# Attention and mixture-of-experts layer on one Trainium2 core: the written-out orders of its five engines replaced by other orders of the same steps

## Chip, cores and metric

One Trainium2 chip, one of its cores. The metric is the device time of one execution in microseconds (us), the median of several runs. The kernel before has a median of 611.8 us over 3 runs.

## The reference

The input is x of 8 batches, 512 tokens, 128 channels, float32. One layer is computed:

```python
x = x + attention(layernorm(x), wq, wk, wv, wo, head_dirs, scale)
x = x + moe(layernorm(x), ...)

# attention: 16 heads, queries and keys of 3 channels, values of 8, causal
scores = einsum('bhtd,bhsd->bhts', q3, k3) * scale + q_on_dir[..., :, None] * k_on_dir[..., None, :]
out = einsum('bhts,bhsd->bhtd', softmax(where(causal, scores, -inf)), v) @ wo

# moe: one shared expert for every token and the best 2 of 8 experts, hidden width 512
shared = gelu(xf @ Wfc_s + bfc_s) @ Wproj_s + bproj_s
routed = sum over e of (gelu(xf @ Wfc[e] + bfc[e]) @ Wproj[e] + bproj[e]) * gate[:, e]
```

## The kernel before

**Steps.** The work is cut into steps, each a few instructions of one engine. A step is written as kind.b.n, with b a batch (or a group of batches in the expert part) and n a part. Five tables give the order in which each engine issues its steps: TENSOR_ORDER (TensorE, PE in the profile), SCALAR_ORDER (ScalarE, ACT), VECTOR_ORDER (VectorE, DVE), POOL_ORDER (GpSimd, POOL) and SYNC_ORDER (SyncE, SP, which only issues DMAs). In the first, "@place" names the PSUM bank or banks of the step, out of 8: `HB.1.5@5` is in bank 5, and a score step with two pairs of banks has two digits, `E.7.6@64` being banks 4, 5 and banks 6, 7. One place, as in `M.3.1@0`, means banks 0 and 1 for most score steps.

**Attention of one batch.** S1 and N1 normalize (DVE, POOL), T1 and XE transpose, QKV projects. QK splits queries and keys into three bfloat16 parts (DVE), SK and SQ spread them (POOL), TK, TQ, KE and QE transpose them, and the DMA step KP writes keys into a padded tile. Softmax maxima come first: each M step (matmuls of L1382 and L1384) writes scores to PSUM, and the MX step of the same number (DVE, L1062) reduces them to `negmax`; 24 of them a batch. PT (L1071 to L1073) splits the maxima of a head group, TM and QM put them into the queries. Then E (L1396, L1404) computes scores with the maxima subtracted, EX (ACT, L920) takes the exponential, MK (POOL, L789) masks, PV (L1423) multiplies by the values, and OE, TP, DV, TO, HE, PJ and RS bring the result back to `acc`.

**Expert part.** S2, N2, T2, X2, RL, LG, LX, RT, RK and RC route a batch: RT picks two experts, RK and RC (L1139 to L1145) give each token a row in a table, SC (POOL, L813) sends rows there by indirect DMA. The shared expert is H, GS, Y and SA; BS (POOL, L800) adds its bias. Batches form three groups of 5, 2 and 1. TB (DVE, L1154 to L1170) makes the group's table of blocks from the counts that CT (L1474) adds up. Then come 47, 23 and 15 blocks of 128 rows: WC (SP, L627) loads the 578 KB of a block's weights into one of 6 `wcur` buffers, XB (SP, L640) a pair of blocks' rows into one of 2 `xblk` buffers, XT and XV transpose, HB (L1502) and GB (ACT, L958) are the first product and the gelu, YB (L1510) and YE (DVE, L1241) the second, YS (SP, L647) stores the pair. GA (POOL, L827) fetches rows back and CB (DVE, L1258) adds them. The last group is summed on TensorE instead (SB on DVE, CM on PE, L1526). OU (SP, L652) stores results.

**What sets the order.** Every engine issues its table's steps strictly in order, and a step waits with semaphores for what it reads. The waits come out of the tables: `counted()` numbers the steps of each kind as the tables have them, and `banks_before()` finds for each PE step who held its banks before, and `wait_taken` waits until that was read:

```python
for kind, b, n, place in TENSOR:
    for unit in sorted(BEFORE.get((kind, b, n), ())):
        wait_taken(unit)
...
elif kind == "HB":
    pe.wait_ge(gelu_blk, nth("GB", b, n))
```

So a step on a bank waits for the engine that empties it. SP's queue is in order too: XB behind a WC stands still while that WC waits for its `wcur` buffer:

```python
if k >= NW:
    pg, ps = block_at(k - NW)
    sp.wait_ge(yblk_done, nth("YB", pg, ps))
    sp.wait_ge(yblk_ready, nth("YE", pg, ps // 2))
    sp.wait_ge(gelu_blk, nth("GB", pg, ps))
```

ACT's function tables (ACT_TABLE_LOAD) are loaded whenever an Exp step follows a gelu step or the other way round, so the order in SCALAR_ORDER sets their number.

Of the kernel before, what the change touches and what calls it, by code (L numbers as in the profile page):

```python
# [1657 lines left out]
```

## Time and profile before

| | |
|---|---|
| median of 3 runs | 611.8 us (611.73 to 622.73) |
| the profiled execution | 612.41 us, its span 610.2 us |
| mean granted TensorE clock | 0.988 of full speed |
| busy: PE, PEld, DVE, ACT, POOL | 550.8, 423.7, 436.3, 388.0, 325.1 us |
| DMA | 99.48 MB, mean 163 GB/s |
| chain that ended last | PE 64%, DVE 19%, issue 7%, ACT 4%, DMA 3% |

The span is that of one execution on the core; 2.2 us of its time lie outside it. PE is the matmuls, PEld the weight loads that overlap them. The chain is followed back from the last instruction to whatever released each step.

### The profile page before, as it was taken

How to read it: one execution, taken by the hardware profiler on the slowest of the kernel's cores; microseconds unless marked ns; L12 is line 12 of the kernel's file. 1: busy time of each engine (PE TensorE's matmuls, PEld its weight loads, DVE VectorE, ACT ScalarE, POOL GpSimd, SP SyncE). 2: the span in 40 equal slices, each digit the busy share in tenths (PEclk: the TensorE clock that was granted, in tenths of full speed). 3: DMA queues.
4: the chain of work that ended last, by engine and by line, in shares of the span. 5: the costliest groups of instructions: out<-in, count | busy, mean ns of one | idle time of the engine just before them, and what ended most of it. 6: DMA issues, size and time to landing. Idle time of an engine off the chain costs nothing.

```text
span 610.2 us, 15780 instructions
## 1 busy us (share of the span) xinstructions
PE 550.8 (90%) x5276; PEld 423.7 (69%) x5318; DVE 436.3 (72%) x1147; ACT 388.0 (64%) x685; POOL 325.1 (53%) x434
## 2 busy tenths in 40 slices
PE   2688999998998999999899998999999899998997
PEld 2555556675664756656668887889878678888996
DVE  6799987799889797798974742446653235845888
ACT  5346678675657679758578686857795945543342
POOL 6844635678268576779654222210450574674544
PEclk9999999999999999999999998999999989998999
DMA  6235752031372212002435858577868846797993
GB/s 179 48 98 173 247 179 98 18 105 36 109 197 81 61 34 74 27 28 49 150 106 200 281 164 275 192 226 226 253 204 287 261 149 196 232 338 249 287 286 120
DMA packets 62429, 99.48 MB, mean 163 GB/s; under 512 B 9020, under 2 KB 47840, under 8 KB 61920
## 3 DMA queue, kind: packets, MB, share of 16 engines
q1 hardware_dynamic: 58512, 90.62, 47.7%
q0 software_dynamic: 3840, 7.87, 3.9%
q8 instruction: 44, 0.72, 0.5%
q14 instruction: 33, 0.27, 0.1%
HBM read 83.37 MB, written 31.80 MB: 189 GB/s over the span
## 4 chain that ended last, share of the span: by engine, by line
PE 64%; DVE 19%; issue 7%; ACT 4%; DMA 3%; SPq 1%; POOL 1%; DVEq 0%; ACTq 0%; POOLq 0%
PE banks L1502 11%; PE banks L1510 11%; PE banks L1423 9%; DVE negmax L1062 7%; PE banks L1333 7%; PE banks L1382 7%; PE banks L1384 4%; PE banks L1480 3%; PE banks L1485 3%; DMA xblk<-xs 2%; ACT probs L920 2%; PE banks L1404 2%; PE banks L1352 2%; PE banks L1526 2%; PE banks L1396 1%
## 5 line engine op out<-in xcount | busy, mean ns | idle before, releaser
L1062 DVE TENSOR_REDUCE negmax<-banks 128x2 f32<-128x1024 f32 (+3 forms) x192 | 193.8, 1039 | 42.2 <-PE banks L1384 40.8
L920 ACT ACTIVATE probs<-banks 128x1024 f32<-128x1024 f32 x160 | 155.6, 1025 | 24.9 <-PE banks L1404 17.0
L789 POOL TENSOR_SCALAR_AFFINE_SELECT probs<-probs 128x512 f32<-128x512 f32 x128 | 78.7, 641 | 128.2 <-ACT probs L920 128.1
L958 ACT ACTIVATE hblk<-banks,wcur 128x128 f32<-128x128 f32 x340 | 95.1, 379 | 80.4 <-PE banks L1502 71.5
L1382 PE MATMUL banks<-kpad,qst 128*128 128x256 bf16 (+3 forms) x470 | 104.9, 295 | 3.9 <-DVE negmax L1062 2.1
L1384 PE MATMUL banks<-future,identb 128*128 128x128 bf16 x512 | 95.6, 220 | 8.5 <-DVE negmax L1062 2.6
L1502 PE MATMUL banks<-xblkT,wcur 128*128 128x128 f32 x680 | 93.0, 285 | 10.0 <-issue 5.9
L1502 PEld LDWEIGHTS banks<-xblkT,wcur 128*128 128x128 f32 x680 | 84.8, 197 | 16.2 <-issue 10.0
L1510 PE MATMUL banks<-wcur,hblk 128*128 128x128 f32 x680 | 91.4, 280 | 1.1 <-ACT hblk L958 1.1
L1510 PEld LDWEIGHTS banks<-wcur,hblk 128*128 128x128 f32 x680 | 83.6, 195 | 5.3 <-issue 3.0
L813 POOL DMA_INDIRECT xs<-x2n,row x64 | 64.6, 1009 | 42.4 <-DVE row L1145 17.6
L1382 PEld LDWEIGHTS banks<-kpad,qst 128*128 128x128 bf16 x512 | 50.0, 98 | 39.7 <-DVE negmax L1062 12.2
L827 POOL DMA_INDIRECT got<-ys,from_row x56 | 55.7, 994 | 40.3 <-DVE acc L1258 21.6
L1423 PE MATMUL banks<-probs,vext 128*32 128x512 f32 (+3 forms) x1024 | 75.7, 436 | 0.2 <-issue 0.2
L1423 PEld LDWEIGHTS banks<-probs,vext 128*32 128x32 f32 x1024 | 30.2, 110 | 45.1 <-issue 36.5
L1384 PEld LDWEIGHTS banks<-future,identb 128*128 128x128 bf16 x512 | 50.3, 98 | 3.5 <-issue 2.3
L884 ACT ACTIVATE ot<-banks 128x512 f32<-128x512 f32 x32 | 19.1, 598 | 49.9 <-PE banks L1423 49.9
L1241 DVE TENSOR_TENSOR yblk<-banks,wcur 128x128 f32<-128x128 f32 x85 | 20.6, 284 | 37.8 <-PE banks L1510 34.3
L1226 DVE COPY xblkT<-banks 128x256 f32<-128x256 f32 (+1 forms) x44 | 18.0, 410 | 28.5 <-PE banks L1333 25.1
L1485 PE MATMUL banks<-w2s,hidden 128*128 128x128 f32 x256 | 34.8, 280 | 0.0
L1480 PE MATMUL banks<-x2T,w1s 128*128 128x512 f32 x64 | 32.4, 611 | 0.0
L1485 PEld LDWEIGHTS banks<-w2s,hidden 128*128 128x128 f32 x256 | 31.0, 192 | 1.7 <-issue 1.3
(156 smaller groups left out, 819.5 us busy)
## 6 DMA issues: line engine op xcount, KB each, us to landing
wcur<-wtab SPq DMA_DIRECT2D x85, 578.0 KB, 5.2
xs<-in_L_attn_x SPq DMA_DIRECT2D x8, 1188.0 KB, 7.1
xblk<-xs SPq DMA_DIRECT2D x85, 64.0 KB
ys<-yblk SPq DMA_DIRECT2D x34, 128.0 KB, 4.0
kpad<-kst SPq DMA_DIRECT2D x64, 64.0 KB, 2.1
xs<-in_L_attn_x SPq DMA_DIRECT2D x8, 505.0 KB
acc<-in_L_attn_x SPq DMA_DIRECT2D x8, 256.0 KB, 5.3
wtab<-in_L_ffn_Wfc SPq DMA_DIRECT2D x2, 1024.0 KB
```

Of the source, the lines that this page charges most:

```text
L789: pool.affine_select(out=v, in_=v, compare_op=ALU.is_ge, fill=0.0, base=0, pattern=[[0, R], [1, P]], channel_multiplier=-1).then_inc(maske ...
L813: pool.indirect_dma_start(out=xs[g % 2], out_offset=bass.IndirectOffsetOnAxis(ap=row[:, b % 2, k, i:i + 1], axis=0), in_=x2n[:, b % NX2, i ...
L827: pool.indirect_dma_start(out=got[:, half_of, k, j, :], out_offset=None, in_=ys[g], in_offset=bass.IndirectOffsetOnAxis(ap=from_row[:, b % ...
L920: nc.scalar.activation(probs[:, g % 2, heads[0]:heads[-1] + 1, at:at + P * sum(EUNITS[unit])], src, ACT.Exp).then_inc(exp_done, 1)
L958: ins = nc.scalar.activation(hblk[:, k % 3, q, :], one(PLACE["HB", g, s])[:, P * q:P * q + P], ACT.Gelu_apprx_tanh, bias=wcur[:, k % NW, 2 ...
L1062: dve.tensor_reduce(negmax[:, g, 0, tiles - 1, heads[0]:heads[-1] + 1], unit_view(PLACE["M", b, n], tiles), AX.X, ALU.max, negate=True).th ...
L1382: mm(dst[:, m, :], qst[:, key_place(b, g), g % 2, P * i:P * i + P], kpad[:, key_place(b, g), g % 2, r, 0:P * tiles], start=opens_bank(tile ...
L1384: ins = mm(dst[:, m, P * i:P * i + P], identb[:], future[:], start=False, stop=True, skip_group_check=True)
L1423: ins = mm(banks[W * r:W * r + W, place, P * j:T], vext[:, j, R * g + r, :], probs[:, g % 2, r, PCOL[NT - j]:PCOL[NT - j] + T - P * j], st ...
L1485: ins = mm(one(place)[:, P * i:P * i + P], hidden[:, q, P * i:P * i + P], w2s[:, q, :], start=(q == 0), stop=(q == NQ - 1))
L1502: ins = mm(one(place)[:, P * q:P * q + P], wcur[:, k % NW, P * q:P * q + P], v, start=True, stop=True)
L1510: ins = mm(one(place)[:, at:at + C], hblk[:, k % 3, q, :], wcur[:, k % NW, HID + C * q:HID + C * q + C], start=(q == 0), stop=(q == NQ - 1))
```

## The change

The five tables are replaced. Every step is there once, as before: 781 on TensorE, 393 on ScalarE, 492 on VectorE, 234 on GpSimd, 228 on SyncE. No function changes. TensorE's steps stand 1.6 places away from their old place on average, at most 21; VectorE's 1.5, one of them 60; GpSimd's 2.4, at most 28; SyncE's 2.9, at most 35; ScalarE's 0.7. Most steps on TensorE are also in other PSUM banks. Since ACT's table loads follow from the order, there are 36 of them now, and 34 before.

Four lines of the diff, two of SYNC_ORDER and two of POOL_ORDER, stand for the rest:

```diff
-    WC.1.22 XB.2.0 WC.2.0 XB.2.1 WC.2.1 XB.2.2 OU.0.1 YS.1.8 YS.1.9 WC.2.2 WC.2.3 WC.2.4 YS.1.10 WC.2.5 XB.2.3
...
+    YS.1.8 WC.1.22 OU.0.0 WC.2.0 XB.2.0 YS.1.9 WC.2.1 XB.2.1 WC.2.2 XB.2.2 WC.2.3 WC.2.4 YS.1.11 WC.2.5 XB.2.3
...
-    GA.1.0 GA.1.1 GA.1.3 N2.7.0 GA.2.3 GA.2.1 GA.2.2 GA.2.0 BS.6.0 BS.7.0 SC.7.2 SC.7.0 SC.7.1 SC.7.3 GA.3.0
...
+    GA.1.3 GA.1.0 GA.1.1 GA.1.2 N2.7.0 GA.2.0 GA.2.2 GA.2.3 GA.2.1 BS.7.0 SC.7.2 SC.7.3 SC.7.1 SC.7.0 GA.3.1
```

BS.6.0 now stands before SC.6.2. In VECTOR_ORDER the first PT (PT.0.0) comes behind 14 MX steps, where it came behind 12. In SCALAR_ORDER `X2.6.0 EX.7.5 EX.7.6 LX.6.0 GB.0.34` becomes `X2.6.0 GB.0.34 LX.6.0 EX.7.5 EX.7.6`. In TENSOR_ORDER `CT.2.0@0 HB.1.12@4 H.7.0@7 H.7.3@2 YB.1.11@3 RK.7.0@7 HB.1.13@4 YB.1.12@1 HB.1.14@7` becomes `CT.2.0@7 HB.1.13@5 RK.7.0@4 YB.1.11@0 HB.1.12@3 H.7.0@5 H.7.3@2 YB.1.12@7 HB.1.14@4`.

**Place 1, VectorE in batch 2.** The last two maxima of batch 2 and the first of batch 3 (MX.3.2), with the two PT steps between them (L1071 to L1073). Before:

```order
L1042 TENSOR_TENSOR parts<-rest 128x2x96
L1062 TENSOR_REDUCE negmax<-banks 128x2 x2
L1071 TENSOR_TENSOR negmax<-negmax 128x16
L1072 COPY qrows<-negmax 128x2x4x4
L1073 TENSOR_TENSOR qrows<-negmax 128x4x4
L1071 TENSOR_TENSOR negmax<-negmax 128x16
L1072 COPY qrows<-negmax 128x2x4x4
L1073 TENSOR_TENSOR qrows<-negmax 128x4x4
L1062 TENSOR_REDUCE negmax<-banks 128x2
L1139 TENSOR_TENSOR row_of<-banks,first_row 128x32
```

and now:

```order
L1042 TENSOR_TENSOR parts<-rest 128x2x96
L1062 TENSOR_REDUCE negmax<-banks 128x2 x2
L1139 TENSOR_TENSOR row_of<-banks,first_row 128x32
L1140 TENSOR_TENSOR row_hot<-hot,row_of 128x64
L1141 TENSOR_REDUCE row_f<-row_hot 128x8
L1145 CAST row<-row_f 128x8
L1071 TENSOR_TENSOR negmax<-negmax 128x16
L1072 COPY qrows<-negmax 128x2x4x4
L1073 TENSOR_TENSOR qrows<-negmax 128x4x4
L1062 TENSOR_REDUCE negmax<-banks 128x2
L1248 TENSOR_TENSOR acc<-banks,acc 128x512
```

The pair of reductions was MX.2.21 and MX.2.15 and is now MX.2.21 and MX.3.2; the step that frees the bank of M.3.2 has moved ahead of both PT steps.

**Place 2, TensorE at the end of batch 7's attention.** L1404 is E.7.6 here, L1423 is PV.7.3, the L1502 rows are blocks of group 1. Before:

```order
L1480 MATMUL banks<-x2T,w1s 128x512
L1502 MATMUL banks<-xblkT,wcur 128x128 x4
L1404 MATMUL banks<-qmst,kpad 128x512 x4
L1502 MATMUL banks<-xblkT,wcur 128x128 x4
L1333 MATMUL banks<-ident,xblk 128x128 x2
L1502 MATMUL banks<-xblkT,wcur 128x128 x8
L1423 MATMUL banks<-probs,vext 32x512 x4
```

and now:

```order
L1502 MATMUL banks<-xblkT,wcur 128x128 x4
L1480 MATMUL banks<-x2T,w1s 128x512
L1502 MATMUL banks<-xblkT,wcur 128x128 x4
L1404 MATMUL banks<-qmst,kpad 128x512 x4
L1423 MATMUL banks<-probs,vext 32x512 x4
L1423 MATMUL banks<-probs,vext 32x384 x4
L1423 MATMUL banks<-probs,vext 32x256 x4
L1423 MATMUL banks<-probs,vext 32x128 x4
L1502 MATMUL banks<-xblkT,wcur 128x128 x4
```

HB.1.4 has moved ahead of E.7.6, and HB.1.5, which stood ahead of PV.7.3, behind it.

**Place 3, SyncE in group 1.** The weights of blocks 1.10 and 1.11 (L627) and the first rows of pair 1.7 (L640). Before:

```order
L627 DMA wcur<-wtab 128x1156
L647 DMA ys<-yblk 128x2x128
L626 TENSOR_LOAD block_of
L626 ISA x2
L627 ISA
L627 DMA wcur<-wtab 128x1156
L639 TENSOR_LOAD block_of
L639 ISA x2
L640 ISA
L640 DMA xblk<-xs 128x128
```

and now, with the weights of block 1.9 in the first row and those of 1.10 in the last:

```order
L627 DMA wcur<-wtab 128x1156
L639 TENSOR_LOAD block_of
L639 ISA x2
L640 ISA
L640 DMA xblk<-xs 128x128
L639 TENSOR_LOAD block_of
L639 ISA x2
L640 ISA
L640 DMA xblk<-xs 128x128
L626 TENSOR_LOAD block_of
L626 ISA x2
L627 ISA
L627 DMA wcur<-wtab 128x1156
```

The loads of pair 1.7 now come before those of the weights of 1.10 and 1.11, which they followed.

## Rows read from the trace of the kernel before

**Rows 1.** The page: busy time of the engines, and the chain's engines.

```profile
PE 550.8 (90%) x5276; PEld 423.7 (69%) x5318; DVE 436.3 (72%) x1147; ACT 388.0 (64%) x685; POOL 325.1 (53%) x434
...
PE 64%; DVE 19%; issue 7%; ACT 4%; DMA 3%; SPq 1%; POOL 1%; DVEq 0%; ACTq 0%; POOLq 0%
```

**Rows 2.** Windows: length; busy PE, PEld, DVE, ACT, POOL; granted clock; DMA share; GB/s.

```profile
0.00:20.00 20.00, 6.38 (x25) 4.87 (x25) 15.13 (x46) 8.75 (x8) 14.46 (x37) 1.00 0.52 146
...
40.00:50.00 10.00, 5.96 (x69) 3.83 (x69) 9.75 (x20) 7.03 (x9) 5.15 (x7) 1.00 0.39 139
...
140.00:150.00 10.00, 9.35 (x97) 6.51 (x95) 9.55 (x34) 6.61 (x8) 8.91 (x12) 1.00 0.15 42
150.00:160.00 10.00, 7.63 (x77) 5.11 (x80) 8.41 (x25) 2.72 (x4) 3.46 (x5) 0.83 0.11 28
...
490.00:500.00 10.00, 10.00 (x99) 6.69 (x98) 2.99 (x9) 5.10 (x18) 6.64 (x9) 0.85 0.44 129
...
540.00:550.00 10.00, 10.00 (x91) 9.94 (x90) 4.95 (x15) 6.24 (x19) 6.84 (x8) 1.00 0.99 344
```

**Rows 3.** Timeline of PE, its long idle times: start, us, instructions, idle before.

```profile
152.32 0.31 PE L1384 MATMUL banks<-future,identb 128*128 128x128 bf16 x1 [2.57 <-DVE negmax L1062]
...
377.50 2.05 PE L1502 MATMUL banks<-xblkT,wcur 128*128 128x128 f32 x8 [2.64 <-ACT hblk L958]
...
489.16 3.41 PE L1502 MATMUL banks<-xblkT,wcur 128*128 128x128 f32 x16 [1.94 <-issue]
...
513.72 0.41 PE L1333 MATMUL banks<-ident,xblk 128*128 128x128 f32 x2 [1.51 <-DMA xblk<-xs]
...
529.87 1.16 PE L1502 MATMUL banks<-xblkT,wcur 128*128 128x128 f32 x8 [1.39 <-DVE row L1145]
...
553.13 0.41 PE L1333 MATMUL banks<-ident,xblk 128*128 128x128 f32 x2 [2.55 <-DMA xblk<-xs]
```

**Rows 4.** Timelines of DVE and POOL from 145 to 151 us.

```profile
146.98 2.09 DVE L1071 TENSOR_TENSOR negmax<-negmax 128x16 f32<-128x16 f32 x1
...
150.92 0.94 DVE L1062 TENSOR_REDUCE negmax<-banks 128x2 f32<-128x768 f32 x1
...
146.26 2.90 POOL L766 COPY krows<-parts 128x576 bf16<-128x576 bf16 x3
```

**Rows 5.** Line L1071 in the whole trace: min/median/max in ns.

```profile
L1071 DVE TENSOR_TENSOR negmax<-negmax x32: 156/167/2091, 38.7 to 465.5; 128x16 f32<-128x16 f32 x32
```

**Rows 6.** Timelines of ACT and SP from 480 to 488 us.

```profile
482.02 5.74 ACT L920 ACTIVATE probs<-banks 128x1024 f32<-128x1024 f32 x6
...
480.29 1.75 SPq L640 DMA_DIRECT2D xblk<-xs  x2
482.90 1.68 SPq L627 DMA_DIRECT2D wcur<-wtab  x2
```

**Rows 7.** The chain from 503 to 514 us: start, us, what.

```profile
503.77 0.50 DVE yblk L1241 x2
...
508.92 4.67 DMA xblk<-xs
```

**Rows 8.** Timelines of DVE and POOL from 524 to 528 us.

```profile
524.33 3.06 DVE L1161 SCALAR_TENSOR_TENSOR end_row<-used,end_row 1x8 f32<-1x8 f32 x1
...
524.87 2.49 POOL L800 TENSOR_TENSOR acc<-acc,b2s 128x512 f32<-128x512 f32 x2
```

**Rows 9.** Timeline of SP from 544 to 549 us.

```profile
544.70 0.34 SPq L627 DMA_DIRECT2D wcur<-wtab  x1
545.89 1.44 SPq L640 DMA_DIRECT2D xblk<-xs  x2
```

**Rows 10.** Timeline of ACT from 435 to 441 us.

```profile
435.62 0.60 ACT L884 ACTIVATE x2T<-banks 128x512 f32<-128x512 f32 x1 [1.06 <-PE banks L1333]
438.33 1.94 ACT L920 ACTIVATE probs<-banks 128x1024 f32<-128x1024 f32 x2 [2.11 <-PE banks L1404]
...
440.40 1.28 ACT L958 ACT_TABLE_LOAD   x1
```

More of the change, by code:

```diff
@@ new lines @@
+    M.3.11@1 M.3.5@7 TQ.3.1@6 E.2.5@4 M.2.16@2 TK.3.1@0 M.2.12@6 M.2.23@1 E.2.1@24 QKV.4.0@0 M.2.14@6 M.2.18@2
+    T2.1.0@1 M.2.22@4 M.2.20@6 RL.1.0@1 H.1.3@3 M.2.19@4 H.1.2@2 H.1.1@1 H.1.0@0 E.2.3@62 M.2.21@4 QKV.4.1@1
+    PV.2.0@0 Y.1.0@7 M.3.2@2 Y.1.1@7 RK.1.0@6 E.2.4@40 Y.1.2@7 M.2.15@2 Y.1.3@7 M.3.0@0 TK.4.0@6 M.3.1@2
+    TK.4.1@7 TM.2.2@5 TM.2.3@4 TP.2.0@6 M.3.3@0 PV.2.1@5 E.2.8@0 M.3.12@2 E.2.6@64 M.3.4@0 E.2.11@2 M.3.14@6
+    TP.2.1@5 M.3.17@4 E.2.9@20 M.3.13@6 M.3.16@4 T1.5.0@3 E.2.10@6 M.3.23@2 M.3.15@4 E.2.7@26 M.3.19@0 M.3.7@4
@@ new lines @@
+    M.7.22@4 YB.0.17@6 HB.0.18@1 TP.6.1@6 M.7.0@2 XT.0.10@0 HB.0.19@5 HB.0.20@4 YB.0.18@7 HB.0.21@3 E.6.8@0
+    XT.0.11@6 M.7.20@4 YB.0.19@7 YB.0.20@3 HB.0.22@6 XT.0.12@7 E.6.7@40 YB.0.21@3 HB.0.23@2 M.7.1@4 PV.6.3@7
+    M.7.2@0 XT.0.13@6 HB.0.24@3 YB.0.22@2 M.7.3@0 PV.6.2@6 YB.0.23@2 HB.0.25@6 XT.0.14@2 YB.0.24@3 M.7.7@0
+    TM.7.0@6 M.7.21@4 HB.0.26@7 HB.0.27@6 YB.0.25@3 E.7.0@40 HB.0.28@2 XT.0.15@6 TP.6.3@3 YB.0.26@7 TP.6.2@2
+    HB.0.29@3 YB.0.27@7 TO.6.0@2 M.7.10@4 E.7.2@0 YB.0.28@2 XT.0.16@7 HB.0.31@6 M.7.6@0 HB.0.30@7 M.7.8@4
@@ new lines @@
+    YB.0.29@2 PJ.6.0@3 HB.0.32@6 HB.0.33@7 E.7.1@20 YB.0.30@5 M.7.17@6 XT.0.17@4 YB.0.31@5 M.7.9@6 HB.0.34@4
+    YB.0.32@5 M.7.13@6 TM.7.1@1 T2.6.0@0 M.7.16@2 YB.0.33@5 RL.6.0@0 XT.0.18@7 H.6.3@6 E.7.3@20 HB.0.35@7
+    PV.7.0@5 M.7.14@0 YB.0.34@4 HB.0.36@3 RK.6.0@2 YB.0.35@4 HB.0.37@7 E.7.4@20 YB.0.36@6 E.7.5@4 XT.0.19@7
+    YB.0.37@6 H.6.0@7 HB.0.38@6 CT.1.0@3 HB.0.39@2 XT.0.20@1 H.6.2@0 TM.7.3@1 HB.0.40@5 HB.0.41@4 YB.0.38@6
+    XT.0.21@2 YB.0.39@6 HB.0.42@5 YB.0.40@6 M.7.15@2 YB.0.41@6 YB.0.42@7 XT.0.23@6 HB.0.43@0 XT.0.22@5 PV.7.1@4
@@ new lines @@
+    VS.2.1 XE.3.0 EX.0.4 EX.0.1 EX.0.0 VS.2.0 EX.0.3 EX.0.2 EX.0.9 EX.0.5 EX.0.6 OE.0.0 EX.0.14 EX.0.7 EX.0.8
+    KE.2.0 OE.0.1 EX.0.12 EX.0.13 EX.0.19 EX.0.10 EX.0.11 KE.2.1 QE.2.0 OE.0.2 EX.0.16 EX.0.15 EX.0.18 EX.0.17
+    EX.1.0 EX.1.1 EX.1.4 OE.0.3 EX.1.3 EX.1.2 HE.0.0 EX.1.6 EX.1.5 EX.1.9 OE.1.0 EX.1.14 EX.1.8 EX.1.7 VS.3.0
+    EX.1.10 EX.1.11 X2.0.0 QE.2.1 VS.3.1 EX.1.13 EX.1.12 OE.1.1 LX.0.0 GS.0.3 GS.0.2 GS.0.1 GS.0.0 OE.1.2
+    EX.1.15 EX.1.16 EX.1.19 EX.1.18 EX.1.17 KE.3.0 OE.1.3 QE.3.0 HE.1.0 XE.4.0 EX.2.0 EX.2.1 EX.2.4 QE.3.1
@@ new lines @@
+    MX.0.11 MX.0.2 MX.0.13 MX.0.5 MX.0.0 MX.0.8 MX.0.16 MX.0.14 PT.0.0 MX.0.10 QM.0.0 MX.0.18 QK.2.1 PT.0.1
+    MX.0.12 QM.0.1 QK.2.0 MX.1.5 MX.0.15 MX.0.17 MX.0.23 PT.0.2 MX.0.19 MX.1.11 S1.4.0 QM.0.2 MX.1.0 DV.0.0
+    MX.0.22 MX.1.4 MX.1.3 MX.0.21 MX.0.20 PT.0.3 MX.1.1 MX.1.2 QM.0.3 DV.0.1 MX.1.12 MX.1.17 MX.1.23 MX.1.14
+    MX.1.18 MX.1.13 PT.1.0 MX.1.16 QM.1.0 DV.0.2 MX.1.6 MX.1.9 MX.1.15 MX.1.8 PT.1.2 MX.1.10 MX.1.7 PT.1.1
+    QM.1.1 DV.0.3 MX.1.20 MX.1.22 QM.1.2 RS.0.0 S2.0.0 MX.2.4 MX.1.19 MX.1.21 PT.1.3 MX.2.1 DV.1.0 QK.3.0
@@ L241 @@
+    YS.1.10 WC.2.6 XB.2.4 WC.2.7 WC.2.8 XB.2.5 OU.2.0 WC.2.9 OU.0.1 WC.2.10 WC.2.11 WC.2.12 OU.3.0 WC.2.13
+    XB.2.6 OU.2.1 OU.5.1 OU.4.1 XB.2.7 OU.4.0 OU.5.0 WC.2.14 OU.1.1 OU.3.1 OU.6.1 OU.6.0 OU.7.1 OU.7.0
 """
```

287 lines of the change are left out of this document (130 added, 157 removed).

## Prediction

> **What bounds the kernel now.** I read the page's busy times first, then the chain by engine, windows of 10 us, the idle times of TensorE in its timeline, and around each of the long ones the timelines of the engine that it waited for. TensorE is the bound: busy 550.8 us of a span of 610.2, and 64% of the chain [rows 1]. Its instructions stay, so what an order can win is the other 59.4 us, and the time lost at the lower clock. Of the 59.4, 13.6 lie in the first 20 us (20 less 6.4 busy) [rows 2], where data arrive and nothing else can be done. Six of the long idle times add up to 2.57 + 2.64 + 1.94 + 1.51 + 1.39 + 2.55 = 12.6 us [rows 3]. The other 33 us are in many mostly small pieces, 4.0 of them between 40 and 50 us [rows 2]. Behind some of the long ones the clock falls: in the windows from 150 and 490 us the granted clock averages 0.83 and 0.85 [rows 2]. With levels of 1.2 and 2.4 GHz, 0.83 means a third of 10 us at the lower, in which half of the work is lost: 1.7 us; at 0.85, 1.5 us. So a long idle time costs up to 1.7 us more than it lasts.
>
> The profiled execution took 612.41 us, 0.6 more than the median of 611.8. I sum against 612.4 and subtract 0.6 at the end.
>
> **The change part by part.** The tables reorder everything a little, so I go to the long idle times and ask what each would find.
>
> *A, at 152 us.* TensorE waits 2.57 us for a reduction of DVE [rows 3]: M.3.1 needs bank 0, which MX.3.2 empties. MX.3.2 ran at 150.92, behind two PT steps, the first of which had L1071 take 2.09 us [rows 4], where its median is 0.167 [rows 5]. Now MX.3.2 directly follows MX.2.21, at about 147 us, ahead of both. That removes at most 2.57 us of idle time and 1.7 of clock, 4.3; at least nothing, since DVE is busy 9.55 of the 10 us before [rows 2] and may be late with the next reduction instead. I take half, -2.1.
>
> *B, at 489 us.* HB.1.5 waits 1.94 us [rows 3] for something the profile doesn't name. Its bank was free when ACT's six Exp ended at 487.76, so for the last 1.4 us I read it as its weights, loaded from the issue at 482.90, behind the `xblk` loads at 480.29 [rows 6]. Now WC.1.5 stands ahead of that XB, worth 1.75 us of issue; HB.1.4 moves ahead of E.7.6, and PV.7.3 ahead of HB.1.5, so that TensorE has work in the gap. The idle time should go, and of 1.5 us of clock I count 1.0, since smaller gaps just before stay. -2.9, between 0 and -3.4.
>
> *C, at 513.7 us.* XT.1.7 waits 1.51 us for rows [rows 3]. The chain shows why: YE (503.77) released WC.1.10, and XB.1.7, behind it and WC.1.11, landed at 508.92 + 4.67 = 513.59 [rows 7]. Now XB.1.7 is ahead of both and waits for no YE. -1.2, between 0 and -1.5.
>
> *D, at 529.9 us.* HB.1.14 waits 1.39 us for RC.7.0 [rows 3], which follows TB.2. In TB.2 one tiny DVE operation took 3.06 us and ended with POOL's two bias additions of 2.49 us together [rows 8], BS.6.0 and BS.7.0. BS.6.0 is gone from there, so half of the 2.49, 1.2 us, is saved, and between RK.7.0 and HB.1.14 stand five PE steps instead of two. -1.1, between 0 and -1.4.
>
> *E, at 553 us.* XT.2.0 waits 2.55 us for rows [rows 3], issued at 545.89, 1.2 us behind weights at 544.70 [rows 9]. Here the change goes the wrong way: WC.2.0 and OU.0.0 now also stand ahead of XB.2.0. That is 1.2 + 0.4 us of issue, and up to 1.7 us to move 578 KB at the 344 GB/s of this stretch [rows 2]. Against it TensorE gets two more steps of 8 matmuls and two transposes to do before XT.2.0, 2.1 us (such a step shows 1.16 us in [rows 3], 0.2 of it filling the array). Between 1.6 - 2.1 = -0.5 and 3.3 - 2.1 = +1.2; I take +0.4.
>
> *F, the start.* PT.0.0 comes two MX steps later, so the first E and Exp come up to some 2 us later, at 0.94 us for a narrow reduction [rows 4]; the reductions done earlier are not needed later, so most comes back. +0.5, between -0.5 and +2.0.
>
> *G, two more table loads on ACT,* 1.28 us each [rows 10], near 437 us. ACT was idle there 1.06 + 2.11 us for TensorE [rows 10], which covers 2.6. Nothing, and 2.6 us if that cover is gone.
>
> *At 377 us* (2.64 us, for a gelu of ACT) the three blocks, the two parts of Y and the M step ahead of the first step that needs this gelu are the same as before. Nothing.
>
> *H, what the new order brings of its own.* A and D show what a table cannot know well: a small DVE operation held up by POOL. At other places it will happen again. One such event with the clock behind it costs 2.6 + 1.7 = 4.3 us, as at 152 us; I give it a chance of 0.6, +2.6. Bounds: none, and two (8.6). The 33 us of small pieces I leave as they are; a fifth of them, 6 us, could go.
>
> In the Trainium skill, SBUF: State Buffer, "SBUF: two separate sides", a DVE operation with two inputs in SBUF and a GpSimd operation that reads SBUF exclude each other, and the second blocks until the first instruction is through. The rows agree in kind and not in size: L1071, with both inputs in SBUF, was held 1.9 us while POOL made three copies in 2.90 us [rows 4], which is two copies and not one. By the rule such an event costs 1.0 us less, H would be +2.0, and the sum 0.6 us lower.
>
> The sum: -2.1 - 2.9 - 1.2 - 1.1 + 0.4 + 0.5 + 0 + 2.6 = -3.8 us. 612.4 - 3.8 - 0.6 = 608.0 us.
>
> **Rivals.** *R1, the gain is paid back.* TensorE is 90% busy and DVE 72%, with 9.55 of 10 us before the longest stall, and in the last 100 us the DMA share comes to 0.99 [rows 2]. An engine so full meets the next wait as soon as one goes. For it: DVE at A, DMA at E. Against it: at B and C what was late was only the place in a queue. The gains of A to D (7.3) shrink to 3, H and E + F stay at 3.5: 611.8 + 0.5, about 612.
>
> *R2, slower, by DVE operations that POOL holds up.* The mechanism of A and D at new places: PT and RT are chains of small DVE operations on the way to E and to the expert rows, and POOL's copies, masks and additions have moved by 2.4 places. With two such events (8.6), half of A to D (-3.6) and E + F (+0.9), +5.9: 617.7. It decides from the second event on. For it: both seen events fell at long waits of TensorE. Against it: L1071 has a median of 0.167 us over 32 times, so it was held badly once [rows 5].
>
> *R3, the longer search really is better everywhere.* No new event, A to D in full (-10.6), the small pieces less by 2, E + F at +0.9: -11.7, 600.1. For it: four of the six long stalls have steps moved ahead of exactly what they wait for. Against it: I looked only where the old order was bad; the new one's bad places aren't in this trace.
>
> *R4, the operations don't quite stay as they are.* 36 table loads against 34: if at 437 us and later ACT is what TensorE waits for, the forecast and 2.6 us, 610.6.
>
> **How the numbers follow.** Forecast (605 to 610) 0.42; R1 0.28; R3 0.13; R2 0.12; R4 0.05. The range for 8 in 10: low end, A to D in full (-10.6), E and F at their lower bounds (-1.0) and no new event, -11.6: 600.2; high end, A to D by half (-3.6), E and F at their upper bounds (+3.2) and one event (4.3), +3.9: 615.7. A measurement of this kernel tells about 2% from no change, 12.2 us: under 599.6 or over 624.0. Faster by more than that is the better half of R3, 0.07; slower by more needs three or four events, 0.02; the rest, 0.91, is within 2%.
>
> **What would show it.** Right: in the new trace no wait of TensorE over 1 us near 150, 489 and 514 us; TB.2 with end_row near 1.4 us or less; TensorE's idle time at about 55 us with the same busy time and 36 table loads; XT.2.0 still waiting 2 to 3 us for its rows. R1: the long waits gone and as much idle time in small pieces. R2: a new wait over 1.5 us for DVE, with a DVE operation of 16 or 32 elements over 1 us beside a POOL copy or mask. Wrong altogether: idle time under 48 us, or a long wait at a place that none of A to H names.

## The result and the profile after

| | before | changed |
|---|---|---|
| median of 16 runs | 608.7 us (604.4 to 622.7) | 605.5 us (601.8 to 607.3) |
| ratio of the changed kernel to before | | 0.9937, 95% interval 0.9914 to 0.9959 |
| the profiled execution | 612.41 us, span 610.2 | 604.5 us, span 602.2 |

The change makes the kernel 0.63% faster, which is within 2% and yet outside the noise. The ratio compares fast runs alone, without the slow 622.7 us run of before; the two medians give 0.9947. The prediction said 608.0 us, a change of -0.6% from 611.8. The size of the change was met: 0.6% off the 608.7 us that 16 runs of before give, instead of the 611.8 of the first three, would have been 604.9. But the terms behind it missed in both directions, as the experiments show.

The page of the changed kernel, busy times and the chain by engine, answering to [rows 1]:

```profile
PE 553.6 (92%) x5318; PEld 421.1 (70%) x5318; DVE 439.3 (73%) x1147; ACT 389.3 (65%) x687; POOL 326.2 (54%) x434
...
PE 63%; DVE 16%; issue 7%; ACT 5%; DMA 4%; SPq 3%; POOL 2%; DVEq 0%; POOLq 0%; ACTq 0%
```

TensorE is idle 602.2 - 553.6 = 48.6 us. The trace of before lacks 42 of its 5318 matmuls, so its 59.4 us are too many. A second trace of the same kernel (e4) has all of them, a span of 608.0 and 553.2 busy: 54.8 us idle. From there the idle time falls by 6.2 us and the span by 5.8: between these two executions it is idle time that the new order wins.

Windows of the changed kernel (columns as in [rows 2]); the two at 200 and 290 us are new in the list:

```profile
40.00:50.00 10.00, 7.90 (x69) 5.46 (x66) 9.45 (x22) 6.97 (x9) 1.11 (x2) 0.90 0.01 2
140.00:150.00 10.00, 10.00 (x99) 6.72 (x98) 9.46 (x39) 7.30 (x9) 9.00 (x12) 1.00 0.06 15
150.00:160.00 10.00, 9.73 (x111) 6.30 (x110) 9.72 (x23) 6.17 (x7) 7.55 (x9) 1.00 0.36 107
...
200.00:210.00 10.00, 8.20 (x81) 4.66 (x81) 7.88 (x22) 3.97 (x5) 4.74 (x8) 0.83 0.84 244
290.00:300.00 10.00, 7.25 (x69) 4.18 (x69) 8.06 (x36) 4.04 (x6) 5.45 (x7) 0.83 0.06 20
...
490.00:500.00 10.00, 10.00 (x102) 8.39 (x101) 5.02 (x16) 6.46 (x21) 6.69 (x8) 1.00 0.53 141
```

In the window from 150 us TensorE is busy 9.73 of 10 us, against 7.63, and the granted clock is 1.00 there and from 490 us, where [rows 2] have 0.83 and 0.85. The same 0.83 now stands at 200 and 290 us. What is behind it shows in the long idle times of TensorE, its timeline as in [rows 3]:

```profile
204.74 0.45 PE L1404 MATMUL banks<-qmst,kpad 32*128 32x384 bf16 x8 [1.13 <-DVE row L1145]
...
293.01 0.18 PE L1464 MATMUL banks<-chosen,earlier 128*128 128x32 bf16 x1 [2.75 <-DVE sofar L1133]
304.16 0.60 PE L1396 MATMUL banks<-qmst,kpad 128*128 128x256 bf16 x4 [1.79 <-DVE qmst L1080]
380.69 0.41 PE L1333 MATMUL banks<-ident,xblk 128*128 128x128 f32 x2 [1.19 <-DMA xblk<-xs]
520.69 1.13 PE L1502 MATMUL banks<-xblkT,wcur 128*128 128x128 f32 x8 [2.08 <-issue]
549.13 0.41 PE L1333 MATMUL banks<-ident,xblk 128*128 128x128 f32 x2 [0.79 <-DMA xblk<-xs]
...
584.80 0.44 PE L1333 MATMUL banks<-ident,xblk 128*128 128x128 f32 x2 [1.61 <-DVE yblk L1241]
```

None of the six waits of [rows 3] is left in its old size: those at 152, 377, 489, 514 and 530 us are gone, and the last, XT.2.0's, is 0.79 us. The one at 304 us is an old one, 1.51 us at 300.55 in before. The one at 520.69 us is new and recurs in all traces with the new second half (1.94 us in e3, 1.38 in e5, 1.62 in e7, 1.64 in e9, 1.21 in e10, 1.80 in e11, 1.10 in e12). It is HB.1.13, ahead of RK.7.0, and it is for its weights. The trace has the time at which each of a DMA's 16 parts landed: the last part of these weights landed at 520.60, 0.09 us before the matmul. The one at 584.80 us is XT.2.6, which waits for a YE. It is new too, 1.5 to 1.8 us in all eight traces with the new second half and nothing in the six with the old one. Two more are new, at 204 and 293 us. Both come from VectorE operations that take 0.24 us (L1072) and 0.19 (L1111) when nothing holds them. VectorE and GpSimd of the changed kernel around them:

```profile
199.60 2.94 DVE L1072 COPY qrows<-negmax 128x32 bf16<-128x32 bf16 x1
...
198.24 1.28 POOL L800 TENSOR_TENSOR acc<-acc,b2s 128x512 f32<-128x512 f32 x1
199.46 2.98 POOL L789 TENSOR_SCALAR_AFFINE_SELECT probs<-probs 128x512 f32<-128x512 f32 x5
...
285.71 3.98 DVE L1111 TENSOR_TENSOR pr<-pexp,prcp 128x32 f32<-128x32 f32 x1
...
284.52 2.39 POOL L789 TENSOR_SCALAR_AFFINE_SELECT probs<-probs 128x512 f32<-128x512 f32 x4
286.86 2.87 POOL L766 COPY krows<-parts 128x576 bf16<-128x576 bf16 x3
289.62 0.62 POOL L789 TENSOR_SCALAR_AFFINE_SELECT probs<-probs 128x512 f32<-128x512 f32 x1
```

The reader should compare ends. L1072 ends at 202.54 and the five masks at 202.44; L1111 ends at 289.69 and the three copies at 289.73. Each operation was held while several GpSimd operations went by, through the change from masks to copies too. This is term H of the prediction, and it happened twice.

What ends a hold is not the end of GpSimd's row: behind the copies a mask follows without a gap, at 289.62, and L1111 is over all the same. In the kernel before, L1071 ended at 149.07 [rows 4], when GpSimd's masks had just begun:

```profile
149.03 2.47 POOL L789 TENSOR_SCALAR_AFFINE_SELECT probs<-probs 128x512 f32<-128x512 f32 x4
```

How many operations pass before the held one gets its turn, no run here explains.

### The profile page after: what moved, and what is told of

Read it like the earlier page. It is cut to its first block, busy times and chain, and to the rows that moved or that the text cites. A ratio compares the mean times of both kernels' runs of the same rounds, so it can differ in the third digit from the quotient of the medians.

```text
span 602.2 us, 15820 instructions
## 1 busy us (share of the span) xinstructions
PE 553.6 (92%) x5318; PEld 421.1 (70%) x5318; DVE 439.3 (73%) x1147; ACT 389.3 (65%) x687; POOL 326.2 (54%) x434
## 4 chain that ended last, share of the span: by engine, by line
PE 63%; DVE 16%; issue 7%; ACT 5%; DMA 4%; SPq 3%; POOL 2%; DVEq 0%; POOLq 0%; ACTq 0%
PE banks L1423 11%; PE banks L1510 9%; PE banks L1502 9%; PE banks L1382 8%; PE banks L1333 7%; DVE negmax L1062 6%; PE banks L1480 4%; PE banks L1384 3%; PE banks L1485 3%; PE banks L1404 2%; ACT probs L920 2%; PE banks L1352 2%; DMA xblk<-xs 2%; PE banks L1396 2%; PE banks L1442 1%
## 5 line engine op out<-in xcount | busy, mean ns | idle before, releaser
L1062 DVE TENSOR_REDUCE negmax<-banks 128x2 f32<-128x768 f32 (+3 forms) x192 | 193.3, 1039 | 35.9 <-PE banks L1384 35.4
L1382 PE MATMUL banks<-kpad,qst 128*128 128x256 bf16 (+3 forms) x512 | 116.1, 303 | 6.5 <-DVE negmax L1062 2.4
L1502 PE MATMUL banks<-xblkT,wcur 128*128 128x128 f32 x680 | 89.9, 278 | 5.2 <-issue 3.5
L1510 PE MATMUL banks<-wcur,hblk 128*128 128x128 f32 x680 | 90.1, 278 | 0.7 <-ACT hblk L958 0.7
L1502 PEld LDWEIGHTS banks<-xblkT,wcur 128*128 128x128 f32 x680 | 82.0, 192 | 10.5 <-issue 6.2
L1510 PEld LDWEIGHTS banks<-wcur,hblk 128*128 128x128 f32 x680 | 82.1, 192 | 4.5 <-issue 3.5
L1423 PE MATMUL banks<-probs,vext 128*32 128x512 f32 (+3 forms) x1024 | 78.8, 450 | 0.0
L1423 PEld LDWEIGHTS banks<-probs,vext 128*32 128x32 f32 x1024 | 30.9, 112 | 45.7 <-issue 37.0
```

What stands on the lines that cost most here:

```text
L1062: dve.tensor_reduce(negmax[:, g, 0, tiles - 1, heads[0]:heads[-1] + 1], unit_view(PLACE["M", b, n], tiles), AX.X, ALU.max, negate=True).th ...
L1382: mm(dst[:, m, :], qst[:, key_place(b, g), g % 2, P * i:P * i + P], kpad[:, key_place(b, g), g % 2, r, 0:P * tiles], start=opens_bank(tile ...
L1423: ins = mm(banks[W * r:W * r + W, place, P * j:T], vext[:, j, R * g + r, :], probs[:, g % 2, r, PCOL[NT - j]:PCOL[NT - j] + T - P * j], st ...
L1502: ins = mm(one(place)[:, P * q:P * q + P], wcur[:, k % NW, P * q:P * q + P], v, start=True, stop=True)
L1510: ins = mm(one(place)[:, at:at + C], hblk[:, k % 3, q, :], wcur[:, k % NW, HID + C * q:HID + C * q + C], start=(q == 0), stop=(q == NQ - 1))
```

## The experiments

The ratios below are to runs of the kernel before on the same chip, with 95% intervals. Where two changed kernels are compared, it is by these ratios.

### e4, the kernel before once more

> The kernel before once more, for a second trace of it. Theory (long waits are set by the order): TensorE again waits over 2 us near 152 us behind an L1071 of over 1.5 us, over 2 us near 377, over 1 us near 489, 514 and 530 us, and L1161 again takes over 2 us. Rival (they are chance): at least two of the five are under 0.7 us.

610.28 us, span 608.0. TensorE's long idle times:

```profile
152.62 0.39 PE L1382 MATMUL banks<-kpad,qst 128*128 128x512 bf16 x1 [2.17 <-DVE negmax L1062]
...
375.45 1.13 PE L1502 MATMUL banks<-xblkT,wcur 128*128 128x128 f32 x8 [1.58 <-ACT hblk L958]
...
489.91 3.59 PE L1502 MATMUL banks<-xblkT,wcur 128*128 128x128 f32 x16 [2.53 <-issue]
...
529.19 1.16 PE L1502 MATMUL banks<-xblkT,wcur 128*128 128x128 f32 x8 [1.34 <-DVE row L1145]
```

Four of the five recur, with sizes that differ by up to 1.1 us; the one at 514 us is 0.15. L1071 again took 2.095 us at most, but L1161 only 0.154, and in its place another operation of TB.2 was held (VectorE and GpSimd of e4):

```profile
525.26 2.86 DVE L1169 TENSOR_TENSOR block_f<-block_f,block_rows 1x15 f32<-1x15 f32 x1
...
525.59 2.50 POOL L800 TENSOR_TENSOR acc<-acc,b2s 128x512 f32<-128x512 f32 x2
```

So most long waits belong to the order, with a spread of about 1 us each, and which tiny operation is held does not always repeat. Neither expectation holds as it stands: the wait near 377 us is 1.58 us, not over 2. The first trace of before was an unlucky one: of XT.2.0's 2.55 us and 514's 1.51, 0.16 and 0.15 are left. Its clock was unlucky too. It fell behind the waits at 152, 377 and 489 us and behind XT.2.0's, in e4 only behind that at 489 and one of 1.84 us at 468; in e4 the window from 150 us has a granted clock of 1.00.

### e8 and e1, the named edits put into the kernel before

e8 is edit A alone, on VectorE; e1 has B, C and D as well.

```diff
-    ... QK.4.1 MX.2.21 MX.2.15 PT.2.3 PT.2.2 MX.3.2 RC.1.0
+    ... QK.4.1 MX.2.21 MX.3.2 MX.2.15 PT.2.3 PT.2.2 RC.1.0
```

> The kernel before with edit A alone, MX.3.2 directly behind MX.2.21. e1, with all four edits, gained 0.5%, but showed 1.96 us of wait at 151 us again, now of an E step. Theory (A only moves the wait; the gain of e1 is B's and C's): within 1 us of before, and a wait of 1.5 to 2.5 us between 148 and 156 us. Rival (A gains as forecast): 2 us or more less than before.

0.9990 (0.9965 to 1.0016): A alone gives nothing that can be measured, as the theory said. Its trace, TensorE and then VectorE:

```profile
149.98 0.40 PE L1404 MATMUL banks<-qmst,kpad 32*128 32x384 bf16 x8 [1.96 <-issue]
...
148.06 1.82 DVE L1062 TENSOR_REDUCE negmax<-banks 128x2 f32<-128x768 f32 x2 [0.82 <-PE banks L1384]
149.79 0.30 DVE L1071 TENSOR_TENSOR negmax<-negmax 128x16 f32<-128x16 f32 x1
```

L1071 is no longer held (0.30 us) and stands behind both reductions, and yet TensorE waits 1.96 us, now with an E step. VectorE idles 0.82 us for the scores of MX.3.2, which TensorE computes after those of MX.2.15, and ends both reductions at 149.88; the E step starts at 149.98. In the changed kernel the steps of TensorE and MX.2.15 are moved too, and the window from 140 us is full. That A works only with these counterparts fits, but no run adds them one by one.

e1 adds: on TensorE and ScalarE the steps from HB.1.2 to HB.1.10 as the changed kernel has them (YB.1.6 in bank 2), and

```diff
-    ... WC.1.4 XB.1.3 WC.1.5 WC.1.6 XB.1.4 XB.1.5 ... WC.1.9 WC.1.10 YS.1.1 WC.1.11 XB.1.7 XB.1.8
+    ... WC.1.4 WC.1.5 XB.1.3 XB.1.4 WC.1.6 XB.1.5 ... WC.1.9 XB.1.7 WC.1.10 YS.1.1 WC.1.11 XB.1.8
...
-    ... SC.6.0 MK.7.4 SC.6.1 SC.6.3 ... GA.2.0 BS.6.0 BS.7.0 SC.7.2
+    ... SC.6.0 MK.7.4 SC.6.1 BS.6.0 SC.6.3 ... GA.2.0 BS.7.0 SC.7.2
```

> Kernel before with edits A to D alone: MX.3.2 behind MX.2.21 on VectorE; the steps of TensorE and ScalarE from HB.1.2 to HB.1.10 and WC.1.5 ahead of XB.1.3 as in the changed kernel; XB.1.7 ahead of WC.1.10; BS.6.0 behind SC.6.1. Theory (the prediction's terms A to D are what the change gains): 4 to 9 us less than before, the waits at 152, 489 and 514 us under 1 us, end_row (L1161) at most 1.9 us. Rival (the gain is paid back at the next wait): at most 3 us less, with as much idle time of TensorE in other pieces. Rival (the gain of the change lies in places that A to D do not name): within 1 us of before.

0.9953 (0.9929 to 0.9977), 2.9 us: less than the theory's 4 to 9. With e8 at 0.9990, B, C and D together are worth 0.37%, 2.3 us (0.1 to 4.4, from the two intervals). The waits at 489, 514 and 530 us are gone; the one at 152 us is there as in e8, 1.96 us. In the same stretch two others stand:

```profile
533.91 1.13 PE L1502 MATMUL banks<-xblkT,wcur 128*128 128x128 f32 x8 [1.35 <-issue]
...
575.43 0.41 PE L1333 MATMUL banks<-ident,xblk 128*128 128x128 f32 x2 [1.15 <-DMA xblk<-xs]
```

Neither is new. The first is HB.1.17, which waits for its weights: 1.39 us in the first trace of before, 1.48 in e4 and 0.91 in e8. The second is XT.2.5, 0.43, 0.72 and 0.77 us there. So the trace shows little of the rival's payback, and TensorE's idle time is 602.2 - 553.1 = 49.1 us, 5.7 less than in e4.

D can be read on its own by setting e8, where BS.6.0 and BS.7.0 still stand together, beside e1. VectorE and GpSimd of e8, in the table TB.2:

```profile
517.89 3.25 DVE L1167 TENSOR_TENSOR reached<-reached,unused 1x120 f32<-1x120 f32 x1
...
518.49 2.50 POOL L800 TENSOR_TENSOR acc<-acc,b2s 128x512 f32<-128x512 f32 x2
```

and of e1:

```profile
520.05 1.61 DVE L1160 TENSOR_TENSOR end_row<-first_row,skipped 1x8 f32<-1x8 f32 x1
...
520.35 1.28 POOL L800 TENSOR_TENSOR acc<-acc,b2s 128x512 f32<-128x512 f32 x1
```

With two additions some operation of TB.2 takes 3.06 us (L1161, [rows 8]), 2.86 (L1169, e4) or 3.25 (L1167); with one it takes 1.61 (L1160), and HB.1.14 no longer waits (1.43 us in e8). Which operation is held changes; that one is held does not, in these four traces.

### e2, e3, e5, e6 and e9, halves of one order with halves of the other

Each table is cut where both orders have done the same steps: at about 304 us (TensorE behind E.5.7), and for e9 at about 445 us (TensorE behind H.6.3, VectorE behind RT.6.0). The edit is the table's second part, taken from the other kernel. In e5 and e6 the banks of the second part are also turned by one pair (`@4` becomes `@2` or `@6`), so that the seam finds its banks free.

> New orders up to about 304 us (TensorE to E.5.7, the attention of batches 0 to 5), old orders behind. In the two traces the table of group 0 (TB.0.0, L1164) comes at 295.9 us before and 299.6 after, so the new first half looks 3.7 us slower, by VectorE operations held up by GpSimd at 200 us (L1072, 2.94 us) and 286 us (L1111, 3.98 us). Theory (these are set by the order and recur): 2 to 4 us more than before, both operations over 2 us again. Rival (they are chance of one execution, and A's 4.3 us are gained): 2 to 4 us less than before.

> Old orders up to about 304 us, new ones behind. The changed kernel's own 3.8 us (0.6%) are front plus back. Theory: the back gains 6 to 8 us (the stalls at 377, 489, 514 and 530 us gone), 600 to 603 us where before has 608.7, and so this kernel beats the changed one by 2 to 4 us. Rival (the front brings half by A): 2 us less than before and slower than the changed kernel.

> The kernel of e2 (new orders to about 304 us, old ones behind) with the banks turned likewise. e2 took 13 us more than before, with waits of TensorE of 2.4, 2.0 and 1.8 us from 304 to 318. Theory (the new first half is 2 to 4 us slower for the two VectorE operations held by GpSimd, the rest of e2 was the seam): 2 to 4 us more than before, L1072 and L1111 again 2.9 and 4.0 us. Rival (the new first half is no slower): within 1 us of before or less.

> The kernel of e3 (old orders to about 304 us, new ones behind) with the banks of the second part turned by one pair, so that its first steps find their banks free. e3 lost 2 us of TensorE's busy time from 280 to 320 us and 2.4 from 320 to 360 at the seam. Theory (the new second half is the better one, the seam cost e3 its gain): 4 to 6 us less than before. Rival (the new second half gains only because the new first half hands over another state): within 1.5 us of before, as e3.

> Old orders up to about 445 us (TensorE to H.6.3, VectorE to RT.6.0), new ones behind; at this place both orders hold the same banks and nearly the same steps. In the traces the stretch from TB.1.0 to TB.2.0 takes 73.1, 72.4 and 66.9 us with old orders there (before, e4, e8) and 64.0, 64.2, 63.9, 63.9 with new ones (after, e3, e5, e7), and from TB.2.0 to the end 82.8, 84.0, 83.3 against 81.9, 82.1, 81.1, 81.0. Theory (the change gains in this stretch and loses 2 to 3 us up to TB.0.0): 5 to 9 us less than before, a ratio of 0.985 to 0.992, faster than the changed kernel. Rival (the late stretch gains only from the state that the new order hands to it, as the seams of e2, e3, e5 and e6 did the other way): 0.995 to 1.0.

| kernel | to 304 us | behind | ratio to before |
|---|---|---|---|
| e2 | new | old | 1.0222 (1.0193 to 1.0251) |
| e6 | new | old, banks turned | 1.0194 (1.0150 to 1.0237) |
| e3 | old | new | 1.0019 (0.9991 to 1.0047) |
| e5 | old | new, banks turned | 1.0018 (0.9994 to 1.0042) |
| e9 | old to 445 us | new | 0.9975 (0.9944 to 1.0006) |
| changed | new | new | 0.9937 (0.9914 to 0.9959) |

I expected the halves to add up. Of the theories nothing came true but the recurrence: L1072 and L1111 took 2.941 and 3.966 us in e2 and 2.941 and 3.967 in e6. In e5 and e9 the rival held, in e2, e3 and e6 neither did. New front and old back cost 2%, old front and new back 0.2%, and both new gain 0.6%. The banks at the seam explain little of it (1.0222 against 1.0194). In e6 the time goes where the first blocks run:

```profile
313.55 0.40 PE L1404 MATMUL banks<-qmst,kpad 32*128 32x512 bf16 x4 [1.78 <-ACT kst L884]
...
350.39 0.41 PE L1333 MATMUL banks<-ident,xblk 128*128 128x128 f32 x2 [1.98 <-DMA xblk<-xs]
361.32 1.16 PE L1502 MATMUL banks<-xblkT,wcur 128*128 128x128 f32 x8 [2.18 <-DVE yblk L1241]
376.52 3.84 PE L1423 MATMUL banks<-probs,vext 128*32 128x512 f32 x24 [1.99 <-issue]
```

Four waits of 7.9 us together, for ScalarE, a DMA, VectorE and something unnamed, come behind the two of H, which are there as in the changed kernel (1.12 and 2.73 us). The engines arrive at the blocks in another relation to each other than the old second half was made for. That reading is argued from these rows; no run isolates it. It also means that the traces' stretch times, from which I expected 5 to 9 us of e9, were no measure of what a stretch is worth.

### e7, e10, e11 and e12, mending the changed kernel

e7 keeps the two held operations away from GpSimd's runs:

```diff
-    ... MX.4.1 MX.4.3 MX.4.6 RT.2.0 MX.4.7 DV.3.0 PT.3.3 MX.4.5 PT.4.0 RC.2.0 SA.2.0 MX.4.10 QM.3.3 S1.7.0
+    ... MX.4.1 MX.4.3 PT.3.3 MX.4.6 RT.2.0 MX.4.7 DV.3.0 MX.4.5 RC.2.0 QM.3.3 S1.7.0 MX.4.10 SA.2.0 PT.4.0
...
-    MK.5.0 SC.3.2 MK.5.5 MK.5.2 MK.5.4 MK.5.6 SK.7.0 MK.5.7 BS.4.0 SC.4.2 SC.4.1 SQ.7.0
+    MK.5.0 MK.5.5 MK.5.2 MK.5.4 MK.5.6 SC.3.2 MK.5.7 SC.4.2 SC.4.1 SK.7.0 BS.4.0 SQ.7.0
```

> The changed kernel with the steps around the two held operations moved: on VectorE PT.3.3 and PT.4.0 to where the kernel before has them (twelve steps from LG.2.0 on), on GpSimd SC.3.2 behind MK.5.6, SK.7.0 and BS.4.0 behind SC.4.1. Theory (both operations are held until GpSimd's run of back-to-back operations ends, and each costs TensorE its wait and the lower clock behind it): L1111 under 1.5 us and L1072 under 1.3 us at most, the wait of 2.75 us at 293 us under 1 us, 3 to 6 us less than the changed kernel, a ratio to before of 0.984 to 0.989. Rival (DVE is behind anyway, and TensorE waits for the next of its results): 0.992 to 0.996 with the operations short.

1.0004 (0.9973 to 1.0035), slower than the changed kernel, which neither expectation had, although the operations are short: L1111 takes 0.562 us at most and L1072 1.101. VectorE, GpSimd and TensorE of e7:

```profile
297.22 4.99 DVE L1167 TENSOR_TENSOR reached<-reached,unused 1x376 f32<-1x376 f32 x1
...
297.50 2.91 POOL L766 COPY krows<-parts 128x576 bf16<-128x576 bf16 x3
300.25 1.31 POOL L800 TENSOR_TENSOR acc<-acc,b2s 128x512 f32<-128x512 f32 x1
301.45 0.43 POOL L772 MEMSET qrows<- 128x192 bf16 x1
...
304.57 1.01 PE L1396 MATMUL banks<-qmst,kpad 128*128 128x256 bf16 x4 [5.68 <-DVE qmst L1080]
```

The copies that had held L1111 now hold L1167 of the table TB.0.0, which works on one partition, for 4.99 us, and QM.5.3 stands behind the table. The wait at 293 us is gone, and the one at 304 has grown from 1.79 to 5.68. A second wait, 2.63 us at 206 us, is for SA.2.0, which this edit had moved back. Against the changed kernel these two waits are 5.4 us more.

e10 is the changed kernel with the table moved out of QM.5.3's way:

```diff
-    ... MX.6.1 PT.5.3 TB.0.0 QM.5.3 MX.6.23 MX.6.4 MX.6.0
+    ... MX.6.1 PT.5.3 QM.5.3 MX.6.23 MX.6.4 TB.0.0 MX.6.0
```

> The changed kernel with TB.0.0 on VectorE moved from ahead of QM.5.3 and MX.6.23 to behind MX.6.4. In every trace so far an E step waits near 300 us for QM.5.3, which stands behind the table of group 0: 1.5 us in the kernel before, 1.8 in the changed one, 5.7 in e7, where L1167 of that table was held 5.0 us. Theory: that wait goes, 1.5 to 3.5 us less than the changed kernel (ratio to before 0.988 to 0.992). Rival (the M steps behind wait for VectorE instead, or the first blocks come later): the same as the changed kernel within 1 us, with a wait for negmax behind 304 us or a later first block.

1.0060 (1.0035 to 1.0086): 1.2% slower than the changed kernel, for one step moved by three places. Both expectations failed.

```profile
306.59 1.03 PE L1396 MATMUL banks<-qmst,kpad 128*128 128x256 bf16 x4 [5.74 <-DVE block_of L1170]
```

This E step, E.5.11 in banks 6 and 7, now waits 5.74 us for L1170, the last line of the table. The code says why: CT.0.0 wrote its counts to bank 7, and `wait_taken` counts a CT's bank as free only when its whole TB is done. The releaser at 304 us that the profile names in the other traces, L1080, was only the later of two conditions. I had read the wait as one for QM.5.3 alone.

e11 joins the two: e10's table, e7's GpSimd steps, and of e7's VectorE steps only PT.3.3, with PT.4.0 behind SA.2.0.

> e10 with the GpSimd steps of e7 (SC.3.2, MK.5.7, SK.7.0, BS.4.0), and PT.3.3 behind MX.4.3, PT.4.0 behind SA.2.0 on VectorE. Theory (e7 cured L1111 but handed the hold to L1167 ahead of QM.5.3; with the table behind QM.5.3 no one waits for it): 3 to 6 us less than the changed kernel, 0.983 to 0.989 of before. Rival (a hold always finds another operation that TensorE waits for): 0.99 or more, with a new VectorE operation of 16 to 376 elements over 1.5 us and a wait of TensorE behind it.

0.9993 (0.9967 to 1.0018). The ratio is the rival's, its mechanism is not: no new VectorE operation is held, but with the table late, E.5.11 waits 8.24 us for its bank. There is no wait of 0.8 us or more from 47 to 224 us, so that half of the mend is right.

e12 leaves the table in its place and gives it no GpSimd run to meet:

```diff
-    ... LG.2.0 MX.4.1 MX.4.3 MX.4.6 RT.2.0 MX.4.7 DV.3.0 PT.3.3 MX.4.5 PT.4.0 RC.2.0 SA.2.0
+    ... LG.2.0 MX.4.1 MX.4.3 PT.3.3 MX.4.6 RT.2.0 MX.4.7 DV.3.0 MX.4.5 RC.2.0 SA.2.0 PT.4.0
...
-    MK.5.0 SC.3.2 MK.5.5 MK.5.2 MK.5.4 MK.5.6 SK.7.0 MK.5.7 BS.4.0 SC.4.2 SC.4.1 SQ.7.0 MK.5.8 MK.5.14 SC.4.0
+    MK.5.0 MK.5.5 MK.5.2 MK.5.4 MK.5.6 SC.3.2 MK.5.7 SC.4.2 SC.4.1 SC.4.0 SK.7.0 SQ.7.0 BS.4.0 MK.5.8 MK.5.14
```

> The changed kernel with six steps moved: PT.3.3 behind MX.4.3 and PT.4.0 behind SA.2.0 on VectorE (e11 had no wait of 0.8 us at 200 us with these), and on GpSimd MK.5.5 to MK.5.6, SC.3.2, MK.5.7, SC.4.2, SC.4.1, SC.4.0, SK.7.0, SQ.7.0, BS.4.0, so that neither RT.4.0 (L1111) nor the table TB.0.0 (L1154 to L1170) meets a run of copies. e7 showed L1111 at 0.56 us and the wait at 293 us gone, but L1167 of TB.0.0 held 4.99 us and TensorE waiting 5.68 us for what stands behind it; e10 showed that the table also holds a bank that E.5.11 wants, so it stays where it is. Theory (a held operation costs TensorE its wait, if its mend hands the hold to no other operation that is waited for): L1111 and L1167 under 1 us, waits at 293 and 304 us under 1 and 2 us, 3 to 7 us less than the changed kernel, a ratio to before of 0.982 to 0.989. Rival (the mends only shift the hold, or what comes later is bound elsewhere): 0.99 or more.

603.3 us, 0.9898 (0.9856 to 0.9940), the lowest ratio of all, 0.4% below the changed kernel; the two intervals overlap, so that it beats the changed kernel is likely and not shown. The ratio lies between what the theory and the rival expected. VectorE and TensorE of e12:

```profile
293.37 0.54 DVE L1167 TENSOR_TENSOR reached<-reached,unused 1x376 f32<-1x376 f32 x1
...
302.50 0.69 DVE L1248 TENSOR_TENSOR acc<-banks,acc 128x512 f32<-128x512 f32 x1 [4.37 <-POOL acc L800]
...
303.25 0.67 PE L1333 MATMUL banks<-identb,krows 128*128 128x128 bf16 x8 [4.39 <-DVE acc L1248]
```

L1111 and L1167 are short, the waits of 1.13, 2.75 and 1.79 us are gone, and the table is 7 us earlier than in the changed kernel (L1164 at 292.2 against 299.6). Then SA.4.0 waits for BS.4.0, which I had put behind the copies, and TensorE waits 4.39 us for SA.4.0: most of the lead is lost at the one step that was moved to make it.

## Why the prediction was right, and where it was not

*What bounds the kernel.* Right. Between e4 and the changed kernel, TensorE's idle time and the span fall by nearly the same amount (6.2 and 5.8 us).

*A, -2.1.* In the changed kernel the whole wait is gone: 4.3 us with its clock by the first trace of before, 2.2 by e4's, where the clock did not fall behind it. By itself the edit gives 0.6 us (-1.0 to 2.1). The step that failed is that "MX.3.2 directly follows MX.2.21" was the reason; the order of TensorE's M steps is as much part of it.

*B, C and D, -2.9, -1.2 and -1.1.* All three waits are gone. B's reading as weights was right: in before, e4 and e8 their last part landed at 489.07, 489.82 and 484.28, and HB.1.5 began 0.09 us later each time; in e1 they landed at 487.63, 1.4 us ahead of it. D's reason is shown by one addition against two. The size failed: 5.2 us were forecast and 2.3 measured (0.1 to 4.4). Over before, e4 and e8 the waits of B, C and D average 1.84, 0.78 and 1.39 us, 4.0 together, and the clock behind B fell in two of the three; I had taken sizes and clock from the slowest of them. Whether small pieces pay back the rest, as R1 has it, stays open. The changed kernel has its own new wait, 2.08 us at 520.69: in the order before, the weights of HB.1.13 lay ready 2.3 us before it.

*E, +0.4.* The forecast wait of 2 to 3 us is 0.79. WC.2.0 and OU.0.0 do stand ahead of the rows now, but this wait is 2.55, 0.16 and 0.73 us in three traces of the old order and 0.58 to 1.64 us in the eight of the new one: one trace was no base for a term.

*At 377 us, "nothing".* This failed, by its reading of the wait. The profile names a gelu, but the step that waits is HB.0.17, and it waits for its weights: their last part landed at 377.41 in before, 375.36 in e4 and 374.52 in e8, each 0.09 us ahead of it. So it is a wait of B's kind. The wait, 2.64, 1.58 and 0.97 us, is gone in the changed kernel, where WC.0.17 stands ahead of XB.0.9 and YB.0.14 ahead of HB.0.17, and 1.19 us for the rows of XB.0.9 stand at 380.69. I had compared only TensorE's steps.

*F, +0.5.* Wrong in sign. The first ranking matmul of batch 0 (L1464) starts at 116.1 us, and at 118.0 in the first trace of before; in all seven traces with the new first half it is 114.6 to 116.1, in the seven with the old one 118.0 to 121.0. In [rows 2]'s window from 40 us the two longest waits fall from 1.12 and 1.54 us to 0.45 and 0.80. Of the rise from 5.96 to 7.90 us busy, with 69 matmuls in both, about 1 us is only the lower clock (0.90 of 10 us, so 2 us at half speed, an estimate).

*G.* 36 table loads, and no wait of TensorE near 437 us. Right.

*H, +2.6.* The mechanism was right and the count wrong: two events, not 0.6 of one. By the trace they cost 1.13 + 2.75 us of wait, and 1.7 us of clock in each of two windows at 0.83: 7.3 us, near the upper bound of 8.6. The waits recur in e2, e6 and e10, so they belong to the new order. That is their cost in the trace; what a mend wins back is less (e12: 0.4%).

So the number stood partly by luck: larger gains (A in full, 377 us, the start, and XT.2.0 by the first trace) met a larger loss (H twice). R2 had the events and too little gain; R3 had the gains and no event. R2's "held badly once" came from the median and the maximum of one line; the same trace holds L1071 a second time (1.38 us at 208 us), and with L1042, L1072 and L1161 it has, after the start, five operations held by more than 1 us, of which two cost a long wait. None of the cases was right part by part.

Of my signs, the waits at 150, 489 and 514 us, TB.2 (L1161 takes 0.154 us) and the 36 table loads came out as in "right". The idle time of 48.6 us instead of 55 and XT.2.0 did not. R2's sign came true as well, L1111 and its 2.75 us. Of the two signs of "wrong altogether", idle time under 48 us was missed by 0.6, but the second came true: HB.1.13's 2.08 us and XT.2.6's 1.61 stand at places that none of A to H names.

On the Trainium skill's rule (SBUF: State Buffer, "SBUF: two separate sides"), by which the second of the two blocks for one instruction of the other: the runs agree that a VectorE operation with its operands in SBUF and a GpSimd operation exclude each other, and not on the length. L1072 was held through five masks, L1111 through the rest of four masks and three copies. Other holds do have the length of one: L1072 of the kernel before took 0.68 us at 149.11, beside one mask of 0.65.

## What to carry to other kernels

An order that was searched as a whole can't be valued by its waits one by one: A alone, or half of the new order, gave nothing or lost up to 2%, while all of it gained 0.6%. The size of a wait, and whether the clock falls behind it, should come from several traces, and its cause from the landing times too: for a step that waits for weights the profile named "issue", a gelu or an Exp. Before a step is moved, ask for all that it holds, its PSUM bank and the steps queued behind it included: a table moved by three places cost 1.2%, since TensorE wanted the bank that it kept. And small VectorE operations on SBUF belong where GpSimd has no long run of operations, in a chain that TensorE doesn't wait for; a mend has to show where the hold goes next.
